# Attention's softmax denominators from one running sum over four key blocks

## The chip, the cores and the metric

The kernel runs on one core of a Trainium2 chip. The metric is device time in microseconds, the median of several runs; smaller is better. Engines are called as the profile calls them: PE is TensorE, DVE is VectorE, ACT is ScalarE, POOL is GpSimd, SP is SyncE (here it only issues DMAs).

## The reference

The program is a masked self-attention followed by a routed and a shared feed-forward layer. The change touches the attention alone:

```python
def _L0_cond_ref(x, mask, Wq, Wo):          # x: (16, 256, 512), mask: (16, 512)
    NH = 8
    B, D, T = x.shape
    dk = D // NH                            # 32
    xt = jnp.transpose(x, (0, 2, 1))
    q = xt @ Wq.T
    qh = q.reshape(B, T, NH, dk).transpose(0, 2, 1, 3)
    scores = scale * jnp.einsum('bhqd,bhkd->bhqk', qh, qh)
    logits = (scores * cmask + (1.0 - cmask) * NEG) * rmask
    attn = jax.nn.softmax(logits, axis=-1)
    ctx = jnp.einsum('bhqk,bhkd->bhqd', attn, qh)
    ...
x = x + _L0_ffn_ref(_L0_cond_ref(x, cond_2048, Wq, Wo), ...)
```

The softmax needs, for each query, the sum of exp(logit - max) over the 512 keys. That sum is the denominator of which this text tells.

## The kernel before

The program has three stages that follow one another: attention (about the first 735 us of the span), experts, shared.

Attention works in 32 units (NU): a unit u is one batch element and four of its eight heads (HG = 4). The keys of a unit are taken in KB = 4 blocks of 128. Scores are held transposed, keys on the partitions and the 512 queries along the row, so the sum over keys is a sum over partitions and over the four blocks.

For each unit, key block kb and head g:
- PE makes the scores of the block (`ps_e`, L557), and, for the unit two further on, the product whose row maximum is wanted (`ps_m`, L562). Both use two banks in turn, g % 2.
- ACT takes the exponential of `ps_e` into the tile `e[kb]` (L337), 512 queries by four heads, 2048 elements in a row.
- DVE takes the maximum of `ps_m` into `maxcol` (L420). PE may be at most two `ps_m` products ahead of it.
- PE multiplies `e[kb]` with the values into `ps_num` (`numerators`, L455): four products, which the trace shows as eight. They are issued one block late: those of block kb stand in block kb + 1, behind its head 1, and those of block 3 in block 0 of the next unit.

The denominators: `add_pair` adds e[1] into e[0] on POOL (all four heads, 2048 elements), and e[3] into e[2], half of the heads (1024 elements) on DVE and half on POOL. PE then multiplies e[0] with ones into `ps_den` (`denominators(u, 0)`, behind the last head of block 3 of the same unit), and e[2] in the same way on top of it (`denominators(u - 1, 1)`, behind the last head of block 1 of the next unit). ACT copies `ps_den` to `den`, DVE takes the reciprocal in four parts in blocks 2 and 3 of that next unit (L386) and then makes c_f = num * den (L391), all in SBUF. Behind c_f, in even units, DVE copies the small logits tile from PSUM to SBUF (L430). At the start of an even unit it makes two rows of the mask, `row_mask` and `row_neg` (L411, L412), one partition of 512 elements each, from SBUF to SBUF.

Every engine runs its own list of instructions strictly in order; what couples them are the semaphores. POOL's list in the step of unit u is: its half of the last add of unit u - 1; c_lo of unit u - 2 (L232, waits for ACT's c_hi, which waits for c_f); the add of e[1] into e[0] (L148); q_lo, qm_hi, qm_lo for the unit four further on (L243, L244, L246, 512 elements each); in odd steps x_lo (L251, 1024 elements). SP's list waits for qm_lo before it issues the next load of x and the next eight stacking DMAs. In odd steps PE makes two groups of six output products (L444), in even steps the transposes and small products of the routing logits. Both kinds of step have one group of six for q (L444).

The order on DVE, written out in its `step`: in blocks 0 to 3 a maximum for each head; behind head 1 of block 1 its half of the last add of unit u - 1; behind heads 1 and 3 of blocks 2 and 3 the reciprocals; behind the last one c_f.

Of the kernel before, what the change touches and what calls it, by code (L numbers as in the profile page):

```python
def attention(nc, ctx, sems, keep, x, mask, wqT, woT, gates, attn):
# [88 lines left out]
    maxrow_in = [sem(f"maxrow_in{n}") for n in range(RING)]  # L90
    stored = [sem(f"stored{n}") for n in range(2)]
    e_mm, m_mm, num_mm, den_mm = sem("e_mm"), sem("m_mm"), sem("num_mm"), sem("den_mm")
    pair_dve, pair_pool = sem("pair_dve"), sem("pair_pool")
    q_mm, v_mm, mt_mm, o_mm = sem("q_mm"), sem("v_mm"), sem("mt_mm"), sem("o_mm")
    e_done, q_done, v_done, mt_done = sem("e_done"), sem("q_done"), sem("v_done"), sem("mt_done")
    num_done, den_done, chi_done, o_done = sem("num_done"), sem("den_done"), sem("chi_done"), sem("o_done")
# [41 lines left out]
            return lo <= RING * i + n + off < hi  # L138
        return True

    def add_pair(eng, u, pair, heads, done):

        k = 2 * pair

        eng.wait_ge(e_done, (KB * u + k + 2) * HG)
        eng.wait_ge(num_mm, KB * u + k + 1)
        into = e[k][:, heads, :]
        eng.tensor_tensor(into, into, e[k + 1][:, heads, :], ALU.add).then_inc(done, 1)  # L148

    block = ctx.enter_context(nc.Block())  # L150

# [60 lines left out]
    def _(pool):  # L212
# [11 lines left out]
        def step(i, n):  # L224
            u = RING * i + n
            if known(i, n, -1):
                add_pair(pool, u - 1, 1, slice(HG // 2, HG), pair_pool)
            if known(i, n, -2):
                w, slot = u - 2, (n - 2) % RING

                upto(pool, chi_done, w + 1)
                pool.tensor_tensor(c_lo[slot][:], c_f[n % 2][:], c_hi[slot][:], ALU.subtract).then_inc(c_split, 1)  # L232
            if known(i, n):
                add_pair(pool, u, 0, slice(0, HG), pair_pool)
            if known(i, n, 4):
                w, par, bp = u + 4, n % 2, n // 2

                upto(pool, q_done, 2 * (w + 1))
                pool.wait_ge(mask_in[bp], 16 * (i + 2))

                if known(i, n, 2):
                    upto(pool, stack_in[(n + 2) % RING], 16 * STACK_DMAS * (i + 1 + (n + 2) // RING))
                pool.tensor_tensor(q_lo[par][:], q_f[par][:], q_hi[par][:], ALU.subtract).then_inc(ql_done, 1)  # L243
                pool.tensor_tensor(qm_hi[par][:], q_hi[par][:], mask_b[bp][:], ALU.mult).then_inc(ql_done, 1)  # L244
                upto(pool, ql_done, 2 * (w + 1))
                pool.tensor_tensor(qm_lo[par][:], q_lo[par][:], mask_b[bp][:], ALU.mult).then_inc(q_split, 1)  # L246
            if n % 2 == 1 and known(i, n, 5):
                w = 2 * i + (n + 5) // 2
                bp = (n + 5) // 2 % 2
                pool.wait_ge(xhi_done, w + 1)  # L250
                pool.tensor_tensor(x_lo[:], x_f[bp][:], x_hi[:], ALU.subtract).then_inc(x_split, 1)  # L251
# [6 lines left out]
    def _(act):  # L258
# [5 lines left out]

        def copy_denominators(i, n):
            w, par = RING * i + n - 1, (n - 1) % 2
            act.wait_ge(den_mm, 2 * (w + 1))
            act.activation(den[par][:], ps_den[:, :], ACT.Copy).then_inc(den_done, 1)  # L268

        def context_high(i, n):  # L270
# [59 lines left out]

        def weights(i, n, kb, g):
            u = RING * i + n
            if g == 0 and kb % 2 == 0:

                upto(act, den_mm, 2 * (u - 1) + 1 + kb // 2)
            act.wait_ge(e_mm, (KB * u + kb) * HG + g + 1)
            act.activation(e[kb][:, g, :], ps_e[g % 2][:, :], ACT.Exp, scale=SCALE).then_inc(e_done, 1)  # L337

# [36 lines left out]
    def _(dve):  # L375
# [27 lines left out]
        def step(i, n):  # L403
# [9 lines left out]
            for kb in range(KB):  # L413
                for g in range(HG):
                    if known(i, n, 2):
                        w, par = u + 2, n % 2
                        dve.wait_ge(m_mm, (KB * w + kb) * HG + g + 1)
                        if kb == 0 and g == 0:
                            upto(dve, mt_mm, w - 1)
                        dve.reduce_max(maxcol[par][:, g * KB + kb:g * KB + kb + 1], ps_m[g % 2][:, :], AX.X).then_inc(max_done, 1)  # L420
                    if g == 1 and kb == 1 and known(i, n, -1):
                        add_pair(dve, u - 1, 1, slice(0, HG // 2), pair_dve)
                    if g % 2 == 1 and known(i, n, -1):
                        normalise(i, n, 2 * kb + g // 2 - KB)
                        if kb == KB - 1 and g == HG - 1:
                            normalise(i, n, PARTS)
# [9 lines left out]
    def _(pe):  # L436
# [19 lines left out]
                                        start=(kb == 0), stop=(kb == KB - 1))  # L456
            last.then_inc(num_mm, 1)

        def denominators(u, pair):

            if pair == 0:

                upto(pe, den_done, u)
            if pair == 1:
                pe.wait_ge(pair_dve, u + 1)
            pe.wait_ge(pair_pool, 2 * u + pair + 1)
            for g in range(HG):
                last = nc.tensor.matmul(ps_den[g * DK:(g + 1) * DK, :], ones[:, :], e[2 * pair][:, g, :],
                                        start=(pair == 0), stop=(pair == 1))
            last.then_inc(den_mm, 1)  # L470

        def turn_values(i, n):
# [65 lines left out]
        def step(i, n):  # L538
# [6 lines left out]
            for kb in range(KB):  # L545
# [7 lines left out]
                for g in range(HG):  # L553
# [23 lines left out]
                    if g == 2 and kb >= 2 and n % 2 == 1 and known(i, n, -3, hi=NU):  # L577
                        out_rows(i, n, kb - 2)
                    if g == 3 and kb == 1 and known(i, n, -1):
                        denominators(u - 1, 1)  # L580
                    if g == 3 and kb == 3 and known(i, n):
                        denominators(u, 0)

        run_units(pe, step, -4, 5)

# [821 lines left out]
```

## Time and profile before

| what | value |
|---|---|
| median of the runs | 2069.23 us (2065.56 to 2070.95, 3 runs) |
| span of the profiled execution | 2067.4 us |
| busy over the whole span | PE 93%, DVE 51%, ACT 35%, POOL 29% |
| busy in 300 to 500 us, inside attention | PE 96%, DVE 82%, ACT 67%, POOL 64% |

Shares over the whole span mix three stages. The attention stage is read from its own stretch, and what sets its pace from the order of time on each engine. A row of the order of time has start, duration, engine, line, operation, tiles; in square brackets stands how long the engine was idle before it and which engine and tile let it go.

### The profile page before, as it was taken

To read this page: it belongs to the slowest core of one execution; us is meant where nothing else is said; L and a number is where in the kernel's file an instruction comes from. 1 tells how busy PE (TensorE), PEld (TensorE's weight loads), DVE (VectorE), ACT (ScalarE), POOL (GpSimd) and SP (SyncE) were. 2 spreads that over 40 slices of the span, in tenths; PEclk is the share of its full clock that TensorE was granted. 3 is DMA by queue.
4 is the path that set the end of the run, shared out by engine and by line. 5 is a ranking of instruction groups with operands and counts; after the bars stand their busy time and mean duration, and the time that the engine had idled before them with its cause. 6 is when DMAs were issued, how large, how long until landed. Compare 5 with 4: busy or idle time off the path is not lost. (4 is left out here: it accounts for less than half of the span.)

```text
span 2067.4 us, 30281 instructions
## 1 busy us (share of the span) xinstructions
PE 1920.6 (93%) x10324; PEld 1418.9 (69%) x10325; DVE 1061.5 (51%) x1723; ACT 720.1 (35%) x1282; POOL 591.3 (29%) x433
## 2 busy tenths in 40 slices
PE   4999999999999836999999999799999999999996
PEld 2444444444444326999999999688888888888885
DVE  3788888787888455344443443444233332424333
ACT  1566666666666512324343332311101010101100
POOL 3556665666565413111111111001010100101010
PEclk9899999999999956999999999899999999999998
DMA  7765757576765033233332322523030211203021
GB/s 126 120 111 98 113 102 125 92 113 95 131 84 73 21 143 125 81 116 110 123 121 73 114 80 81 169 91 102 1 102 20 81 51 51 67 34 101 0 81 41
DMA packets 103041, 184.22 MB, mean 89 GB/s; under 512 B 10560, under 2 KB 31040, under 8 KB 102992
## 3 DMA queue, kind: packets, MB, share of 16 engines
q1 hardware_dynamic: 91952, 147.41, 32.3%
q0 software_dynamic: 11040, 36.18, 5.9%
q8 instruction: 28, 0.46, 0.1%
q14 instruction: 21, 0.17, 0.0%
HBM read 92.03 MB, written 40.37 MB: 64 GB/s over the span
## 5 line engine op out<-in xcount | busy, mean ns | idle before, releaser
L420 DVE TENSOR_REDUCE maxcol<-ps_m 128x1 f32<-128x512 f32 x512 | 337.5, 681 | 138.8 <-PE ps_m L562 133.1
L337 ACT ACTIVATE e<-ps_e 128x512 f32<-128x512 f32 x512 | 297.0, 596 | 188.4 <-PE ps_e L557 187.6
L1234 DVE TENSOR_TENSOR s_h_f<-s_silu,s_ps_u 128x512 f32<-128x512 f32 x88 | 60.6, 688 | 450.6 <-PE s_ps_u L1290 399.1
L148 POOL TENSOR_TENSOR e<-e 128x2048 f32<-128x2048 f32 x64 | 225.6, 3524 | 181.8 <-ACT e L337 181.5
L1202 ACT ACTIVATE s_silu<-s_ps_g 128x512 f32<-128x512 f32 x88 | 52.6, 598 | 608.1 <-PE s_ps_g L1290 600.5
L562 PE MATMUL ps_m<-kside,qside 97*128 97x512 f32 x512 | 224.7, 444 | 33.2 <-DVE maxcol L420 18.9
L1177 POOL DMA_INDIRECT s_chosen<-routed,s_slot_now x64 | 61.0, 952 | 670.0 <-DVE s_total L1265 659.4
L557 PE MATMUL ps_e<-qside,kside 98*128 98x512 f32 x512 | 237.7, 467 | 3.2 <-ACT e L337 2.4
L557 PEld LDWEIGHTS ps_e<-qside,kside 98*128 98x128 f32 x512 | 97.2, 191 | 192.3 <-ACT e L337 159.1
L964 DVE TENSOR_TENSOR e_h_f<-e_silu,e_ps_h 128x256 f32<-128x256 f32 (+1 forms) x108 | 45.1, 418 | 249.0 <-ACT e_silu L831 249.0
L562 PEld LDWEIGHTS ps_m<-kside,qside 97*128 97x128 f32 x512 | 101.0, 197 | 78.9 <-DVE maxcol L420 53.9
L1290 PE MATMUL s_ps_g<-s_x_hi,s_gu_hi 128*128 128x512 f32 x352 | 138.4, 393 | 3.6 <-DVE s_d_lo L1223 3.6
L455 PE MATMUL ps_num<-e,v 128*32 128x512 f32 x1024 | 137.9, 611 | 0.1
L1290 PE MATMUL s_ps_g<-s_x_lo,s_gu_hi 128*128 128x512 f32 x352 | 137.7, 391 | 0.0
L1301 PE MATMUL s_ps_y<-s_d_hi,s_h_hi 128*128 128x512 f32 x352 | 137.7, 391 | 0.0
L1290 PE MATMUL s_ps_g<-s_x_hi,s_gu_lo 128*128 128x512 f32 x352 | 137.6, 391 | 0.0
L1301 PE MATMUL s_ps_y<-s_d_hi,s_h_lo 128*128 128x512 f32 x352 | 137.1, 389 | 0.0
L1301 PE MATMUL s_ps_y<-s_d_lo,s_h_hi 128*128 128x512 f32 x352 | 136.9, 389 | 0.0
L1290 PE MATMUL s_ps_u<-s_x_hi,s_gu_hi 128*128 128x512 f32 x352 | 136.9, 389 | 0.0
L1290 PE MATMUL s_ps_u<-s_x_lo,s_gu_hi 128*128 128x512 f32 x352 | 136.9, 389 | 0.0
L1290 PE MATMUL s_ps_u<-s_x_hi,s_gu_lo 128*128 128x512 f32 x352 | 136.9, 389 | 0.0
L386 DVE RECIPROCAL den<-den 128x128 f32<-128x128 f32 x128 | 119.5, 939 | 17.0 <-ACT den L268 17.0
(203 smaller groups left out, 4040.8 us busy)
## 6 DMA issues: line engine op xcount, KB each, us to landing
routed<-e_y SPq DMA_DIRECT2D x36, 512.0 KB, 2.8
kside<-q_hi SPq DMA_DIRECT2D x64, 256.0 KB
qside<-qm_hi SPq DMA_DIRECT2D x64, 256.0 KB
x_f<-in_x SPq DMA_DIRECT2D x16, 512.0 KB, 3.4
kside<-q_lo SPq DMA_DIRECT2D x32, 256.0 KB
qside<-qm_lo SPq DMA_DIRECT2D x32, 256.0 KB
attn<-xo SPq DMA_DIRECT2D x32, 256.0 KB, 3.3
keep_rows<-attn SPq DMA_DIRECT2D x8, 1024.0 KB, 5.6
```

The lines of the kernel that those rows point to most:

```text
L148: eng.tensor_tensor(into, into, e[k + 1][:, heads, :], ALU.add).then_inc(done, 1)
L337: act.activation(e[kb][:, g, :], ps_e[g % 2][:, :], ACT.Exp, scale=SCALE).then_inc(e_done, 1)
L386: dve.reciprocal(den[par][:, c], den[par][:, c]).then_inc(rd_done, 1)
L420: dve.reduce_max(maxcol[par][:, g * KB + kb:g * KB + kb + 1], ps_m[g % 2][:, :], AX.X).then_inc(max_done, 1)
L455: last = nc.tensor.matmul(ps_num[g * DK:(g + 1) * DK, :], v[n % RING][:, kb, g, :], e[kb][:, g, :], start=(kb == 0), stop=(kb == KB - 1))
L557: nc.tensor.matmul(ps_e[g % 2][:, :], kside[n][:, g, cols], qside[n][:, g, :], start=True, stop=True).then_inc(e_mm, 1)
L562: nc.tensor.matmul(ps_m[g % 2][:, :], qside[s2][0:MAXROW, g, cols], kside[s2][0:MAXROW, g, :], start=True, stop=True).then_inc(m_mm, 1)
L1177: pool.indirect_dma_start(out=chosen[k][s % 2][:], out_offset=None, in_=routed, in_offset=bass.IndirectOffsetOnAxis(ap=slot_now[:, k, s:s ...
L1202: act.activation(silu[:], ps_g[:], ACT.Silu).then_inc(silu_done, 1)
L1234: dve.tensor_tensor(h_f[:], silu[:], ps_u[:], ALU.mult).then_inc(h_done, 1)
L1290: last = nc.tensor.matmul(ps[:], l[:, t, k, m, :], r[:, m, :], start=(c == 0), stop=(c == len(terms) - 1))
L1301: last = nc.tensor.matmul(ps_y[s][:], l[t % 2][:, c], r[:, t, :], start=(t == 0 and m == 0), stop=(t == NI - 1 and m == 2))
```

## The change

One running sum takes the place of two pair sums. e[0] is added into e[1], that into e[2], that into e[3]. The first two adds are POOL's, all four heads. The last is split between DVE and POOL as the second pair was. PE multiplies e[3] alone with ones: one group of denominators instead of two, in the place of the later one. POOL's first add stands where it stood, but now waits for the numerators of block 1 (before: of block 0), since it writes e[1]. Its second add stands behind the three q operations, ahead of x_lo. The last add, on both engines, waits for the second. ACT waits for the sums before it writes the tiles of the next unit.

```diff
-    def add_pair(eng, u, pair, heads, done):
-        k = 2 * pair
-        eng.wait_ge(e_done, (KB * u + k + 2) * HG)
-        eng.wait_ge(num_mm, KB * u + k + 1)
-        into = e[k][:, heads, :]
-        eng.tensor_tensor(into, into, e[k + 1][:, heads, :], ALU.add).then_inc(done, 1)
+    def add_next(eng, u, kb, heads, done):
+        eng.wait_ge(e_done, (KB * u + kb + 1) * HG)
+        eng.wait_ge(num_mm, KB * u + kb + 1)
+        if kb > 1:
+            eng.wait_ge(sum_pool, (KB - 1) * u + kb - 1)
+        into = e[kb][:, heads, :]
+        eng.tensor_tensor(into, into, e[kb - 1][:, heads, :], ALU.add).then_inc(done, 1)
...
             if known(i, n, -1):
-                add_pair(pool, u - 1, 1, slice(HG // 2, HG), pair_pool)
+                add_next(pool, u - 1, 3, slice(HG // 2, HG), sum_pool)
...
             if known(i, n):
-                add_pair(pool, u, 0, slice(0, HG), pair_pool)
+                add_next(pool, u, 1, slice(0, HG), sum_pool)
...
                 pool.tensor_tensor(qm_lo[par][:], q_lo[par][:], mask_b[bp][:], ALU.mult).then_inc(q_split, 1)
+            if known(i, n):
+                add_next(pool, u, 2, slice(0, HG), sum_pool)
...
-            act.wait_ge(den_mm, 2 * (w + 1))
+            act.wait_ge(den_mm, w + 1)
...
-            if g == 0 and kb % 2 == 0:
-                upto(act, den_mm, 2 * (u - 1) + 1 + kb // 2)
+            if g == 0 and kb < KB - 1:
+                upto(act, sum_pool, (KB - 1) * (u - 1) + kb + 1)
+            if g == 0 and kb == KB - 2:
+                upto(act, sum_dve, u)
+            if g == 0 and kb == KB - 1:
+                upto(act, den_mm, u)
...
-                        add_pair(dve, u - 1, 1, slice(0, HG // 2), pair_dve)
+                        add_next(dve, u - 1, 3, slice(0, HG // 2), sum_dve)
...
-        def denominators(u, pair):
-            if pair == 0:
-                upto(pe, den_done, u)
-            if pair == 1:
-                pe.wait_ge(pair_dve, u + 1)
-            pe.wait_ge(pair_pool, 2 * u + pair + 1)
+        def denominators(u):
+            upto(pe, den_done, u)
+            pe.wait_ge(sum_dve, u + 1)
+            pe.wait_ge(sum_pool, (KB - 1) * (u + 1))
             for g in range(HG):
-                last = nc.tensor.matmul(ps_den[g * DK:(g + 1) * DK, :], ones[:, :], e[2 * pair][:, g, :],
-                                        start=(pair == 0), stop=(pair == 1))
+                last = nc.tensor.matmul(ps_den[g * DK:(g + 1) * DK, :], ones[:, :], e[KB - 1][:, g, :], start=True, stop=True)
             last.then_inc(den_mm, 1)
...
                     if g == 3 and kb == 1 and known(i, n, -1):
-                        denominators(u - 1, 1)
-                    if g == 3 and kb == 3 and known(i, n):
-                        denominators(u, 0)
+                        denominators(u - 1)
```

## Rows read from the trace of the kernel before

**Rows 1.** Stages: window, length, busy of each engine, PEclk, DMA share, GB/s.

```profile
300.00:500.00 200.00, 192.30 (x1033) 94.79 (x1032) 164.32 (x226) 134.46 (x249) 128.15 (x64) 0.99 0.66 107
```

**Rows 2.** Order of time, PE, 400 to 445: start, duration, what, idle before.

```profile
405.90 1.06 PE L455 MATMUL ps_num<-e,v 128*32 128x512 f32 x8
...
422.12 1.06 PE L468 MATMUL ps_den<-e,ones 128*32 128x512 f32 x8
...
425.64 1.06 PE L455 MATMUL ps_num<-e,v 128*32 128x512 f32 x8
...
433.42 0.40 PE L557 MATMUL ps_e<-qside,kside 98*128 98x512 f32 x1
433.65 0.40 PE L562 MATMUL ps_m<-kside,qside 97*128 97x512 f32 x1
433.98 1.06 PE L468 MATMUL ps_den<-e,ones 128*32 128x512 f32 x8
...
435.32 0.40 PE L562 MATMUL ps_m<-kside,qside 97*128 97x512 f32 x1
...
438.86 0.50 PE L562 MATMUL ps_m<-kside,qside 97*128 97x512 f32 x1 [0.80 <-DVE maxcol L420]
...
443.73 1.07 PE L468 MATMUL ps_den<-e,ones 128*32 128x512 f32 x8
```

**Rows 3.** Order of time, DVE, around two unit boundaries.

```profile
415.15 1.77 DVE L391 TENSOR_TENSOR c_f<-num,den 128x512 f32<-128x512 f32 x1
...
435.68 1.86 DVE L391 TENSOR_TENSOR c_f<-num,den 128x512 f32<-128x512 f32 x1
...
438.13 3.85 DVE L420 TENSOR_REDUCE maxcol<-ps_m 128x1 f32<-128x512 f32 x6
```

**Rows 4.** Order of time, POOL, the odd unit.

```profile
428.34 1.28 POOL L243 TENSOR_TENSOR q_lo<-q_f,q_hi 128x512 fp32r<-128x512 f32 x1 [0.97 <-ACT q_hi L301]
...
430.94 1.29 POOL L246 TENSOR_TENSOR qm_lo<-q_lo,mask_b 128x512 fp32r<-128x512 f32 x1
...
434.61 2.38 POOL L148 TENSOR_TENSOR e<-e 128x1024 f32<-128x1024 f32 x1
```

**Rows 5.** Order of time, POOL, the boundary behind unit 1.

```profile
99.25 2.38 POOL L251 TENSOR_TENSOR x_lo<-x_f,x_hi 128x1024 fp32r<-128x1024 f32 x1
101.59 2.80 POOL L148 TENSOR_TENSOR e<-e 128x1024 f32<-128x1024 f32 x1
104.34 1.45 POOL L232 TENSOR_TENSOR c_lo<-c_f,c_hi 128x512 fp32r<-128x512 f32 x1
```

**Rows 6.** Order of time, DVE, the same boundary behind unit 1.

```profile
100.65 1.53 DVE L391 TENSOR_TENSOR c_f<-num,den 128x512 f32<-128x512 f32 x1
102.10 2.57 DVE L411 CAST row_mask<-mask_b 1x512 fp32r<-1x512 f32 x1
...
105.99 1.27 DVE L420 TENSOR_REDUCE maxcol<-ps_m 128x1 f32<-128x512 f32 x2
```

**Rows 7.** Groups by form, POOL, 200 to 600: count, busy, mean ns, idle before.

```profile
L148 POOL TENSOR_TENSOR e<-e 128x2048 f32<-128x2048 f32 x19 | 87.3, 4594 | 82.8 <-ACT e L337 82.8
L148 POOL TENSOR_TENSOR e<-e 128x1024 f32<-128x1024 f32 x20 | 47.6, 2381 | 14.4 <-ACT e L337 14.1
```

**Rows 8.** Order of time, PE, unit 1 and the boundary behind it.

```profile
92.71 1.06 PE L455 MATMUL ps_num<-e,v 128*32 128x512 f32 x8
...
106.72 0.79 PE L562 MATMUL ps_m<-kside,qside 97*128 97x512 f32 x1 [3.99 <-DVE maxcol L420]
...
112.83 1.07 PE L468 MATMUL ps_den<-e,ones 128*32 128x512 f32 x8
```

**Rows 9.** Stages, two microseconds behind that boundary; columns as in rows 1.

```profile
106.00:108.00 2.00, 1.28 (x4) 0.91 (x5) 1.71 (x4) 0.00 (x0) 0.00 (x0) 0.50 1.10 157
```

**Rows 10.** Order of time, POOL, the last unit's last add.

```profile
711.87 3.38 POOL L148 TENSOR_TENSOR e<-e 128x1024 f32<-128x1024 f32 x1 [4.08 <-ACT e L337]
```

**Rows 11.** Order of time, PE, the last unit's denominators.

```profile
715.40 1.07 PE L468 MATMUL ps_den<-e,ones 128*32 128x512 f32 x8 [1.80 <-POOL e L148]
```

More of the change, by code:

```diff
@@ L92, in attention @@
     e_mm, m_mm, num_mm, den_mm = sem("e_mm"), sem("m_mm"), sem("num_mm"), sem("den_mm")
-    pair_dve, pair_pool = sem("pair_dve"), sem("pair_pool")
+    sum_dve, sum_pool = sem("sum_dve"), sem("sum_pool")
     q_mm, v_mm, mt_mm, o_mm = sem("q_mm"), sem("v_mm"), sem("mt_mm"), sem("o_mm")
```

## Prediction, made before the change was run

> **What bounds the kernel now.** I read the profile in this order: busy time by stage, the costliest groups, then the order of time on TensorE (PE), VectorE (DVE) and GpSimd (POOL) over two units, and last two odd places, in the first and the last units. Only the attention stage, the first third of the span, is touched. In its middle PE is busy 192.3 of 200 us at a granted clock of 0.99, DVE 164, ScalarE 134, POOL 128 [rows 1]. So PE looks like the bound, and POOL looks like the engine with room. Units repeat in pairs, an even and an odd one, of 41.4 us: 19.74 us from the even unit's key block 1 numerators (405.90) to the odd one's (425.64), and back 21.61, read between the denominator groups at 422.12 and 443.73 [rows 2].
>
> The order of time says where PE's share misleads. Behind the last max product of an odd unit (433.65) comes PE's first denominator group (433.98), one more pair of products, and then a product that waited 0.80 us for DVE's maximum, at 438.86 [rows 2]. DVE at that place goes through c_f = num/den, two mask rows and only then the first maximum of the next unit, 438.13 [rows 3]. That chain hangs on nothing that PE does between 433.65 and 438.86. So at each unit boundary DVE is the last to come, and PE already waits.
>
> The second thing to see is c_f. It takes 1.86 us at 435.68 [rows 3], while POOL's 1024-element add runs from 434.61 to 436.99 [rows 4]: c_f ends 0.55 us after POOL does. The same in the early place: c_f issued at 100.65 takes 1.53 us and ends at 102.18, 0.55 us behind the end of POOL's x_lo (99.25 + 2.38 = 101.63) [rows 5, 6]. So a DVE operation with two inputs in SBUF stands still while POOL runs an add, and the other way round: the POOL add queued right behind x_lo takes 2.80 us instead of 2.38 (+0.42) [rows 5]. At the handoff DVE, which had been waiting, went first, although POOL's next instruction was already queued. Then the mask row takes 2.57 us and the next maximum starts at 105.99: both mask operations lost one POOL instruction each [rows 5, 6]. They take 0.59 us together where POOL is idle (end of c_f at 437.54 to 438.13 [rows 3]).
>
> **The change, part by part.** I time each unit from T, the start of its key block 1 numerators: 425.64 for the odd unit, 405.90 for the even one [rows 2].
>
> *Removed: one denominator group of PE per unit.* Max product to max product across it is 435.32 - 433.65 = 1.67 us; two ordinary steps of 0.23 (433.42 to 433.65) would be 0.46, so the group costs 1.21 us [rows 2]. 32 units give 38.7 us of PE time. But it stands at the boundary, before the product that waits for DVE. It comes off the wait and not off the period: I count it at nothing. What hides it is the chain c_f, masks, first maximum.
>
> *Added: one more 2048-element add of POOL per unit, and the first moved later.* POOL's 2048 add is 4.59 us, the 1024 one 2.38 [rows 7]. The first add now waits for key block 1's numerators, T + 1.06 + about 0.1 = T+1.15, where it waited for block 0's. It ends at T+5.74. Behind it, moved 3 us, stand the three q operations, 3.89 us (428.34 to 430.94 + 1.29) [rows 4]: they end at T+9.63. Their stacking DMAs and the load of x on SP's queue wait for the last of them; the stacks are wanted a unit later, so I count nothing, and if that cover were gone it would be the 3 us once per unit. Then the new add: T+9.63 to T+14.22. Then x_lo (2.38, odd units only), POOL's half of the last add (2.38), c_lo. ScalarE's new waits (weights of block 0 for the first sum, block 1 for the second, and so on) end before the ones reckoned below, except in even units by less than a microsecond, and there PE waits for the denominators anyway.
>
> *Odd unit into even unit.* c_f is ready at 435.68 - 425.64 = T+10.04. The new add has been running since T+9.63, so c_f stands until T+14.22 and ends about 0.55 later. Then the pattern of the early place [rows 5, 6] returns: POOL takes x_lo, the first mask row stands behind it; POOL takes its half of the last add, the second mask row stands behind that. In the early place 4.36 us went from POOL's end (101.63) to the first maximum (105.99) [rows 5, 6] with two POOL instructions of 2.38 and 1.29 in them, so 0.69 over them. Here: 14.22 + 2.38 + 2.38 + 0.69 = T+19.67, against 438.13 - 425.64 = T+12.49 now: +7.2 us. PE, already waiting there, takes all of it. It will stand for some 9 us. In the early place it stood 3.99 us before 106.72 [rows 8], the granted clock behind that was 0.50, the level of 1.2 GHz [rows 9], and from its restart to the denominators took 112.83 - 106.72 = 6.11 us [rows 8], against 443.73 - 438.86 = 4.87 now [rows 2]: +1.2 us. Sum +8.4 us. This happens for odd units 3 to 25, 12 times: 101 us. Unit 1 has no output products yet, so its c_f is ready at 100.65 - 92.71 = T+7.94 [rows 6, 8] and meets the second q operation; the first mask row stands behind the third, the second behind the new add, which ends near 107.5: first maximum at 107.7 where it is 105.99 now, +1.7. After unit 27 there are no masks and no x_lo any more: c_f alone, from T+11.9 to T+14.8, +2.8.
>
> *Even unit into odd unit.* c_f is ready at 415.15 - 405.90 = T+9.25 [rows 2, 3], within the last q operation, which ends at T+9.63. DVE goes first, c_f ends at T+10.18, 0.8 us sooner than now (415.15 + 1.77, T+11.02). The new add loses 0.42 and ends at T+14.64. Both halves of the last add need it, DVE's and POOL's, and they cannot run side by side: in the last unit they start together and the POOL half takes 3.38 instead of 2.38, and the denominators start 715.40 - 711.87 = 3.53 us after that add began [rows 10, 11]. So the denominators come at 14.64 + 0.1 + 3.53 = T+18.27 against 422.12 - 405.90 = T+16.22: +2.05 us, and the 0.8 won is lost in it. 14 such units: 28.7 us.
>
> *Last units (28 to 31).* No q operations, so the new add starts earlier; the removed group is worth 1.21 us in two of them, the last unit's sums are serial and give about 2 us back. Zero, with 5 us either way.
>
> Sum: 101 + 1.7 + 2.8 + 28.7 = 134 us. On the profiled span of 2067.4 that is 2201; the median of the runs is 1.8 above it: **2203 us**.
>
> No row shows the logits copy of even units (PSUM to SBUF, after c_f) beside a POOL add. If it stood too it would cost the even boundary: c_f T+10.2, copy behind the new add at about T+14.8, denominators 5.2 us later at T+20.0 instead of 18.27, +1.7 x 14 = +24 us. Below nothing it can't be. I take zero, since the maxima, which also read PSUM, do not slow beside POOL. The Trainium skill's "VectorE: DVE Perf Modes", section "Why PSUM operands drop a tier", says that the mode of DVE which uses both SBUF read ports is closed to a PSUM operand; by it the price is zero too.
>
> For the handoff the Trainium skill's "SBUF — State Buffer", section "Who interferes with whom", says that issue order decides and the later one blocks fully. It doesn't say who goes next when both have something queued; row 101.59 says DVE [rows 5]. By issue order alone POOL's queued add would be as good a candidate, and that is rival B.
>
> **The rivals.**
> A. c_f gets in ahead of the new add in odd units. The margin is T+10.04 against T+9.63. Then the add ends near T+15.1, the first mask row follows it, the second follows x_lo: first maximum at about T+18.0, 1.6 us less each: 2203 - 19 = 2184.
> B. POOL's queue wins the handoffs. Odd: DVE comes in after x_lo and the last add, T+19.0 + 1.2, +0.5 more than forecast; even: c_f waits through the new add and POOL's half, ends T+17.2, denominators 5.2 later, T+22.4, 4.1 us more. 12 x 0.5 + 14 x 4.1 = 64: 2267. Against it: the add of 101.59, which lost 0.42 us to the waiting c_f [rows 5].
> C. The logits copy stands as well: 2227.
> D. No standing still, only POOL's longer chain: odd T+14.22 + 2.38 + 2.38 + 0.1 = T+19.1 against 18.1 now, +1.0 x 13; even T+16.7 against 16.2, +0.5 x 14: +20, 2089. Against it: c_f's 1.86 us [rows 3].
> E. **Faster**: PE's 96% is what counts and the removed group comes off whole: 2069 - 39 = 2030. Its place is the unit boundary; it decides if DVE's chain there is shorter than PE's, which needs the first maximum to start by T+10.5: PE without its wait and the group would be at the product of 438.86 at 436.85, T+11.2, and a maximum takes 0.7. For it: PE's share [rows 1]. Against it: the 0.80 us that PE waits there already [rows 2], and POOL's 4.6 us right on c_f.
> F. PE's saving turns into wait and nothing else changes: 2069.
>
> **How the numbers follow.** Forecast 0.60, with its own range 2166 to 2236 (12 odd boundaries from 6 to 9.5 us each, clock included, even ones from 1.5 to 3.5). A 0.08, B 0.07, C 0.08, D 0.07, E 0.06, F 0.04. The range of eight in ten takes in the forecast, A, B and C: 2140 to 2268; D, E and F are left out, 0.17. A measurement of this kernel can tell about 0.3% from no change. Faster: 0.06. Same: 0.04. Slower: the rest, 0.90.
>
> **What would show it.** In the changed profile: c_f in odd units near 4.7 us instead of 1.86, and 0.9 in even ones; the first mask row about 2.5 us, the second as long; PE's max product behind the boundary idle some 8 to 9 us before it, by DVE, in odd units; the granted clock at 0.50 after each; POOL's 2048 adds twice as many; the even unit's denominator group waiting 2 to 3 us for the adds; two units taking about 51.8 us instead of 41.4; DVE's half of the last add between 1.2 and 3.5 us. Wrong would be: c_f under 2 us in odd units (D or A), or a first maximum before T+13. The forecast falls with the margin of 0.4 us between the new add and c_f, with the handoff going to POOL, or with a clock that stays down past the denominators (more than 1.2 us per boundary).

## The result, and the profile after

The changed kernel takes 2242.82 us, median of four runs (2241.13 to 2243.49); the kernel before, beside it, 2068.91. The ratio is 1.0843, 95% interval 1.0828 to 1.0857: 174 us slower. The prediction was 2203 us, 134 us slower, with a range of 2140 to 2268. The direction, the mechanism and that range held. The loss was sized 40 us too small: the time lies 7 us above the forecast's own, narrower range of 2166 to 2236, and inside the outer one only because that left room for rival B (2267), which did not come about in this kernel. So that the range held is in part luck. This text is mostly about those 40 us and about a few places where my picture was too simple.

The stage first. A stretch inside attention, columns as in rows 1:

```profile
340.00:540.00 200.00, 150.75 (x742) 78.56 (x740) 153.31 (x177) 105.65 (x195) 146.51 (x59) 0.89 0.50 85
```

PE fell from 192.3 to 150.8 busy of 200 us [rows 1], though it has less to do; DVE from 164 to 153; POOL rose from 128 to 147. The granted clock fell from 0.99 to 0.89. No engine is near full: they wait for one another.

The order of time on PE, an odd unit (T = 414.55) into an even one (T = 444.89):

```profile
411.02 1.06 PE L471 MATMUL ps_den<-e,ones 128*32 128x512 f32 x8 [1.55 <-POOL e L148]
...
414.55 1.07 PE L461 MATMUL ps_num<-e,v 128*32 128x512 f32 x8
...
425.24 0.50 PE L559 MATMUL ps_e<-qside,kside 98*128 98x512 f32 x1
434.89 0.80 PE L564 MATMUL ps_m<-kside,qside 97*128 97x512 f32 x1 [9.15 <-DVE maxcol L426]
...
441.37 1.06 PE L471 MATMUL ps_den<-e,ones 128*32 128x512 f32 x8
...
444.89 1.07 PE L461 MATMUL ps_num<-e,v 128*32 128x512 f32 x8
...
463.06 1.85 PE L471 MATMUL ps_den<-e,ones 128*32 128x512 f32 x8 [1.54 <-POOL e L148]
```

The wait of 0.80 us [rows 2] has become 9.15, and the even unit's denominators, which waited for nothing, now wait 1.54 us for POOL's sum.

DVE, from the end of an even unit to the next even one:

```profile
402.10 0.97 DVE L397 TENSOR_TENSOR c_f<-num,den 128x512 f32<-128x512 f32 x1
402.99 0.16 DVE L436 COPY keep_logits<-ps_o 128x18 f32 x1
...
407.52 1.23 DVE L148 TENSOR_TENSOR e<-e 128x1024 f32<-128x1024 f32 x1 [0.61 <-POOL e L148]
...
424.55 4.73 DVE L397 TENSOR_TENSOR c_f<-num,den 128x512 f32<-128x512 f32 x1
429.20 2.56 DVE L417 CAST row_mask<-mask_b 1x512 fp32r<-1x512 f32 x1
431.69 2.55 DVE L418 TENSOR_SCALAR row_neg<-mask_b 1x512 fp32r<-1x512 f32 x1
434.17 1.27 DVE L426 TENSOR_REDUCE maxcol<-ps_m 128x1 f32<-128x512 f32 x2
```

POOL beside it:

```profile
415.79 4.59 POOL L148 TENSOR_TENSOR e<-e 128x2048 f32<-128x2048 f32 x1 [3.59 <-PE ps_num L461]
...
422.97 1.29 POOL L246 TENSOR_TENSOR qm_lo<-q_lo,mask_b 128x512 fp32r<-128x512 f32 x1
424.22 4.51 POOL L148 TENSOR_TENSOR e<-e 128x2048 f32<-128x2048 f32 x1
428.69 2.79 POOL L253 TENSOR_TENSOR x_lo<-x_f,x_hi 128x1024 fp32r<-128x1024 f32 x1
431.44 2.52 POOL L148 TENSOR_TENSOR e<-e 128x1024 f32<-128x1024 f32 x1
433.92 1.44 POOL L232 TENSOR_TENSOR c_lo<-c_f,c_hi 128x512 fp32r<-128x512 f32 x1
```

Read the two together. The new add starts at 424.22, 0.33 us ahead of c_f. c_f ends at 429.28, 0.55 us behind the end of that add. Each mask row, 0.41 us of work, then stands behind one POOL instruction, and each POOL instruction that follows is 0.14 to 0.4 us longer for having let DVE in first. Compare rows 3 to 6: the pattern that stood once in the kernel before, behind unit 1, now stands behind 12 odd units.

### The profile page after: what moved, and what is told of

It reads as the page before. It is cut to its first block and busy times, and to the rows that moved or that the text cites. A ratio compares the mean times of both kernels' runs of the same rounds, so it can differ in the third digit from the quotient of the medians.

```text
span 2241.2 us, 29944 instructions
## 1 busy us (share of the span) xinstructions
PE 1935.1 (86%) x10068; PEld 1440.1 (64%) x10069; DVE 1155.9 (52%) x1723; ACT 721.7 (32%) x1282; POOL 762.9 (34%) x465
## 5 line engine op out<-in xcount | busy, mean ns | idle before, releaser
L148 POOL TENSOR_TENSOR e<-e 128x2048 f32<-128x2048 f32 (+1 forms) x96 | 392.8, 4092 | 245.5 <-PE ps_num L461 242.9
L564 PE MATMUL ps_m<-kside,qside 97*128 97x512 f32 x512 | 237.1, 468 | 146.4 <-DVE maxcol L426 132.5
L559 PE MATMUL ps_e<-qside,kside 98*128 98x512 f32 x512 | 250.6, 491 | 21.5 <-ACT e L343 20.1
L559 PEld LDWEIGHTS ps_e<-qside,kside 98*128 98x128 f32 x512 | 104.5, 205 | 210.6 <-ACT e L343 151.0
L564 PEld LDWEIGHTS ps_m<-kside,qside 97*128 97x128 f32 x512 | 109.7, 214 | 189.8 <-DVE maxcol L426 163.0
L461 PE MATMUL ps_num<-e,v 128*32 128x512 f32 x1024 | 148.8, 656 | 0.8 <-ACT e L343 0.7
L781 POOL COPY e_now<-e_token_of 128x2 uint32 (+1 forms) x37 | 8.4, 226 | 375.8 <-PE e_ps_t L1000 374.2
```

The source lines that it names most:

```text
L148: eng.tensor_tensor(into, into, e[kb - 1][:, heads, :], ALU.add).then_inc(done, 1)
L461: last = nc.tensor.matmul(ps_num[g * DK:(g + 1) * DK, :], v[n % RING][:, kb, g, :], e[kb][:, g, :], start=(kb == 0), stop=(kb == KB - 1))
L559: nc.tensor.matmul(ps_e[g % 2][:, :], kside[n][:, g, cols], qside[n][:, g, :], start=True, stop=True).then_inc(e_mm, 1)
L564: nc.tensor.matmul(ps_m[g % 2][:, :], qside[s2][0:MAXROW, g, cols], kside[s2][0:MAXROW, g, :], start=True, stop=True).then_inc(m_mm, 1)
```

## The experiments

Eleven kernels, each timed beside the kernel before; ratios are to it, with 95% intervals.

**The kernel before with one denominator group of PE less** (before_one_group). The prediction had counted the removed group at nothing, since it stood in front of a wait.

```diff
-            if g == 0 and kb % 2 == 0:
-
-                upto(act, den_mm, 2 * (u - 1) + 1 + kb // 2)
+            if g == 0 and kb == 0:
+                upto(act, pair_pool, 2 * (u - 1) + 1)
+            if g == 0 and kb == 2:
+                upto(act, den_mm, u)
...
                     if g == 3 and kb == 1 and known(i, n, -1):
                         denominators(u - 1, 1)
-                    if g == 3 and kb == 3 and known(i, n):
-                        denominators(u, 0)
```

With the group some waits change too, as the first lines show, and ACT's copy adds 0.001.

> The kernel before with its first denominator group of PE taken out alone: POOL and DVE add as before, and the product with e[2] stands alone. It leaves key blocks 0 and 1 out of the denominators, and adds 0.001 to them so that none is zero. My theory: the group (1.21 us, 32 times) stood in front of a product that waits for DVE's chain anyway, so its time turns into wait: 2069 us, within 6 us. Rival (PE's share of 96% is what counts): 2069 - 39 = 2030 us. In the profile the product behind the odd boundary would wait 2.0 us for DVE instead of 0.80.

Measured: 2088.96 us, ratio 1.0095 (1.0075 to 1.0116). Neither theory had this: with less to do on PE the kernel is 20 us slower. Its trace, PE behind an odd boundary, and the stages behind it:

```profile
392.92 1.07 PE L456 MATMUL ps_num<-e,v 128*32 128x512 f32 x8
...
406.11 0.51 PE L560 MATMUL ps_m<-kside,qside 97*128 97x512 f32 x1 [1.97 <-DVE maxcol L421]
408.60 1.94 PE L456 MATMUL ps_num<-e,v 128*32 128x512 f32 x8
412.53 1.07 PE L466 MATMUL ps_den<-e,ones 128*32 128x512 f32 x8
```

```profile
404.00:406.00 2.00, 0.14 (x1) 0.00 (x0) 2.00 (x5) 1.08 (x2) 0.62 (x2) 1.00 1.07 290
...
408.00:410.00 2.00, 2.00 (x10) 0.38 (x9) 1.93 (x3) 2.00 (x4) 0.00 (x0) 0.54 1.08 131
```

DVE in the same place:

```profile
405.38 4.01 DVE L421 TENSOR_REDUCE maxcol<-ps_m 128x1 f32<-128x512 f32 x6
```

The wait is 1.97 us instead of 0.80, as expected: the group's 1.2 us did turn into wait. The first maximum stays where it was, at T+12.46 (405.38 - 392.92) against T+12.49 before. But the granted clock, 1.00 in the place of rows 2, is then at 0.54, next to its level of 1.2 GHz, and the numerators group takes 1.94 us instead of 1.06. Over 200 us (340 to 540) the granted clock is 0.95 here against 0.99. It does not fall behind every such wait: here it stays at 1.00 from 348 to 408 us, through waits of 1.99 and 1.44. And once, behind its 0.80 us wait at 395.94, it falls in the kernel before as well (0.50 from 398 to 400).

**The same with five idle products in that place** (one_group_filler). Against before_one_group this puts back PE's activity, and nothing else but PE's wait for the copy of the denominators; the changed waits stay.

```diff
+                    if g == 3 and kb == 3 and known(i, n):
+                        upto(pe, den_done, u)
+                        for r in range(5):
+                            nc.tensor.matmul(ps_den[:, :], wo_hi[:, 0, 0:P], wo_hi[:, :, :].rearrange("p k d -> p (k d)"), start=True, stop=True)
```

> The kernel before_one_group (2089 us) with five products of 128x512 (weights by weights, 1.17 us together) in the place of the removed denominators group. Like it, this kernel leaves key blocks 0 and 1 out of the denominators. Nothing but PE's activity at the boundary is put back. My theory (the removed group cost 20 us by letting PE stand 2.0 us instead of 0.8 behind boundaries, after which the granted clock fell to 0.50): the low stretches go and the time comes back to 2069, within 6 us. Rival (the loss comes from the other waits that this kernel changed): 2089 us.

Measured: 2068.36 us, ratio 1.0001 (0.9991 to 1.0010). The 20 us are gone although the changed waits are still there, and the granted clock is back at 1.00: what cost them was the quiet on PE and the low clock behind it. That the removed product's time is worth nothing at the boundary is shown by before_one_group, where the first maximum did not move. The same 200 us stretch:

```profile
340.00:540.00 200.00, 191.79 (x1009) 104.62 (x1005) 163.90 (x226) 134.79 (x250) 130.63 (x64) 1.00 0.67 108
```

**The changed kernel, PE kept busy through the long wait** (after_filler).

```diff
+                    if g == 2 and kb == 0 and n % 2 == 0 and known(i, n, 0, lo=4, hi=27):
+                        pe.wait_ge(o_done, KT * (2 * i + (n - 4) // 2 + 1))
+                        for r in range(34):
+                            nc.tensor.matmul(ps_o[:, :], wo_hi[:, 0, 0:P], wo_hi[:, :, :].rearrange("p k d -> p (k d)"), start=True, stop=True)
                     if known(i, n, 2):
                         s2 = (n + 2) % RING
```

> The changed kernel with 34 products of 128x512 (weights by weights into a free bank, about 0.23 us each, 7.9 us together) ahead of the product that waits 9.15 us behind odd units 3 to 25: PE works through the wait instead of standing. No other engine does anything else. My theory (part of the loss above the forecast is the clock at 1.2 GHz after the long wait, and it lasts past the denominators): the stretches at 0.50 behind odd boundaries go, from restart to denominators 4.9 us instead of 6.5 to 7.2, and the second low stretch in even units may go with them: 12 x 1.6 to 12 x 3.5 less, 2200 to 2224 us. Rival (the clock costs nothing there, DVE is last): 2243 us; if the filler is itself too long, above that.

Measured: 2228.30 us, ratio 1.0766 (1.0747 to 1.0785), 14.5 us less than the changed kernel. In its trace:

```profile
314.55 7.90 PE L563 MATMUL ps_o<-wo_hi 128*128 128x512 f32 x34
324.02 0.50 PE L568 MATMUL ps_m<-kside,qside 97*128 97x512 f32 x1 [1.57 <-DVE maxcol L426]
...
328.90 1.06 PE L471 MATMUL ps_den<-e,ones 128*32 128x512 f32 x8
```

From restart to denominators 4.88 us, as in the kernel before (4.87 [rows 2]). The gain is less than the 19 to 42 us expected, because this is not so everywhere: from an even unit's denominators to the next odd unit's it takes 28.9 us where the clock holds, which it does in two of the twelve places, and 30.3 or 32.1 in the others. Low stretches stayed behind some of the waits of 1.57 us that the filler leaves open, and behind even units, where PE waits for about 1 and 1.5 us.

**Filler at both waits** (after_filler_both): in addition nine products into `ps_den` ahead of the denominators of even units.

```diff
-        def denominators(u):
+        def denominators(u, fill):
...
             upto(pe, den_done, u)
+            if fill:
+                for r in range(9):
+                    nc.tensor.matmul(ps_den[:, :], wo_hi[:, 0, 0:P], wo_hi[:, :, :].rearrange("p k d -> p (k d)"), start=True, stop=True)
             pe.wait_ge(sum_dve, u + 1)
...
-                        denominators(u - 1)
+                        denominators(u - 1, n % 2 == 1 and known(i, n, -1, lo=2, hi=28))
```

> The changed kernel with filler products at both waits: 34 ahead of the 9.15 us wait behind odd units (as in after_filler), and 9 (2.1 us) ahead of the denominators of even units, which wait 1.55 us for POOL. My theory (what is left over the forecast's waits is the clock alone): units 2 to 27 run at 1.0, an odd to even stretch is 28.9 us and an even to odd one 21.8: 12 x 7.2 + 13 x 2.05 + 8 = 121 us over the kernel before, 2190 to 2200 us; the 9 products may hold the denominators some tenths longer than the wait was. Rival (the low stretches of even units cost nothing, only the odd ones do): as after_filler, 2228 us.

Measured: 2213.08 us, ratio 1.0698 (1.0677 to 1.0719). 2190 to 2200 was expected. The middle of attention is as expected, the ends are not. Its clock there:

```profile
340.00:540.00 200.00, 184.77 (x944) 107.69 (x940) 159.31 (x184) 108.69 (x203) 146.39 (x58) 1.00 0.56 90
```

A pair of units takes 51.1 us there (denominators at 378.19 and 429.26, two odd units), of which 0.4 is filler longer than the wait it fills (the even unit's denominators start 0.46 us behind the end of POOL's add, 0.05 in the changed kernel); 50.7 at full clock against 41.4 before. In the changed kernel a pair takes 53.6 on average (denominators of units 5 and 25 at 228.95 and 764.73, ten pairs). So the clock is worth 2.9 us per pair. PE's wait of 1.57 us behind odd units is as long here as in after_filler, and there the clock fell behind most of them; here, with the even units' wait filled, it held at 1.00 throughout these 200 us. So one wait of that length alone doesn't bring it down; the quiet around it counts too. The low stretches ahead of 148 us and behind 776 us, most of them without filler, stayed, and one at 576 to 584 us.

**The mask rows out of the way** (after_masks_late): the two instructions stand behind DVE's half of the last add.

```diff
-            if n % 2 == 0 and known(i, n, 4):
-                ...
-                dve.tensor_copy(row_mask[bp][:], mask_b[bp][0:1, :]).then_inc(rows_done, 1)
-                dve.tensor_scalar(row_neg[bp][:], mask_b[bp][0:1, :], -NEG, NEG, ALU.mult, ALU.add).then_inc(rows_done, 1)
...
                     if g == 1 and kb == 1 and known(i, n, -1):
                         add_next(dve, u - 1, 3, slice(0, HG // 2), sum_dve)
+                    if g == 1 and kb == 1 and n % 2 == 0 and known(i, n, 4):
+                        ...
```

> The changed kernel with DVE's two mask rows moved from the start of even units to behind DVE's half of the last add (key block 1). My theory (each mask operation stands behind one POOL instruction of 2.4 us, and PE with them): the first maximum behind the odd boundary starts at T+14.8 instead of T+19.7, PE's wait falls from 9.15 us to about 4.2; 4.9 us less in 12 units, and some more if the low clock ends sooner: 2175 to 2185 us. Rival (the masks only stretch because c_f is late, and the denominators hold PE anyway): 2230 to 2243 us.

Measured: 2175.72 us, ratio 1.0532 (1.0501 to 1.0563), 67 us less than the changed kernel. As expected: in its new place a mask row takes 0.41 us, PE's wait behind odd units is 4.17 us.

**c_f with one input in PSUM** (after_c_from_psum).

```diff
-                dve.reciprocal(den[par][:, c], den[par][:, c]).then_inc(rd_done, 1)
+                dve.reciprocal(ps_den[:, c], ps_den[:, c]).then_inc(rd_done, 1)
...
-                dve.tensor_tensor(c_f[par][:], num[par][:], den[par][:], ALU.mult).then_inc(c_done, 1)
+                dve.tensor_tensor(c_f[par][:], num[par][:], ps_den[:, :], ALU.mult).then_inc(c_done, 1)
...
-                    copy_denominators(i, n)
...
-            upto(pe, den_done, u)
+            upto(pe, c_done, u)
```

> The changed kernel with c_f reading the reciprocal from PSUM: the four reciprocals work in place on the denominators' bank, ACT's copy of them goes, and c_f has one input in SBUF. The group of the next unit waits for c_f. My theory (two SBUF inputs are what makes c_f stand): c_f takes about 0.7 us in odd units although the second add runs, but the first mask row then stands behind that add and the second behind x_lo: first maximum at T+17.0 instead of T+19.7, 2.6 us less in 12 units and 0.4 in 14: 2206 us. Rival A (each stall counts by itself, c_f's 4.1 us are simply gone): 2193 us. Rival B (c_f stands behind POOL whatever its operands): 2243 us.

Measured: 2183.11 us, ratio 1.0553 (1.0535 to 1.0570). DVE in an odd unit, T = 346.37:

```profile
356.38 0.69 DVE L396 TENSOR_TENSOR c_f<-num,ps_den 128x512 f32<-128x512 f32 x1
356.99 3.85 DVE L416 CAST row_mask<-mask_b 1x512 fp32r<-1x512 f32 x1
360.77 2.55 DVE L417 TENSOR_SCALAR row_neg<-mask_b 1x512 fp32r<-1x512 f32 x1
363.25 1.27 DVE L425 TENSOR_REDUCE maxcol<-ps_m 128x1 f32<-128x512 f32 x2
```

c_f no longer stands, though POOL's add ran from 356.04 to 360.56: two inputs in SBUF are what makes it stand, and rival B of this expectation is out. The next in line, the mask row, stands in its stead, and the first maximum comes at T+16.9 (17.0 expected). So stalls on one chain don't add: taking one away uncovers the next. The time still fell by 60 us and not by 37; behind the shorter wait fewer stretches at the low clock are seen (granted clock over 200 to 700 us 0.91 against 0.89), but I have not separated the two.

**Both together** (after_both).

> The changed kernel with c_f from PSUM and the masks behind DVE's half of the last add: nothing of DVE stands at the boundary. Left are the removed group and POOL's longer chain, whose two last halves exclude each other. My theory: first maximum at about T+10.7 in odd units, but the denominators wait for POOL: T+20.2 instead of 18.1 in odd units, T+17.9 instead of 16.2 in even ones, 3.7 us per pair, 48 us: 2117 us, up to 2140 with stretches at 1.2 GHz. Rival (with the stall gone the removed product pays): 2030 to 2060 us.

Measured: 2169.18 us, ratio 1.0468 (1.0436 to 1.0501), 52 us more than expected. The boundary is free, PE waits there 0.19 us. The loss moved to the denominators of odd units. DVE, then POOL, then PE:

```profile
361.71 6.77 DVE L148 TENSOR_TENSOR e<-e 128x1024 f32<-128x1024 f32 x1
```

```profile
361.49 2.39 POOL L253 TENSOR_TENSOR x_lo<-x_f,x_hi 128x1024 fp32r<-128x1024 f32 x1
363.83 2.36 POOL L148 TENSOR_TENSOR e<-e 128x1024 f32<-128x1024 f32 x1
366.13 1.28 POOL L232 TENSOR_TENSOR c_lo<-c_f,c_hi 128x512 fp32r<-128x512 f32 x1
```

```profile
368.72 1.94 PE L470 MATMUL ps_den<-e,ones 128*32 128x512 f32 x8 [4.77 <-DVE e L148]
```

DVE's half of the last add stood behind three POOL instructions in a row and ran only when POOL's queue was empty. This is the handoff of rival B of the prediction. It went so in 9 of the 12 odd units 3 to 25 (6.67 to 6.81 us); in the other three DVE got in behind x_lo (3.25 to 3.27 us). DVE had come 0.18 to 0.32 us after x_lo began in the nine and 0.21 to 0.22 in the three, so that does not tell them apart. In the changed kernel c_f, the first mask row and the second came 0.33, 0.40 and 0.24 us or more after the start of a POOL instruction and always got in at its end; so did, in even units of after_second_add_ahead_of_q, a DVE add that came 0.07 us after. What decides is open.

**The last add on DVE alone** (after_both_last_add_on_dve).

```diff
...
-                add_next(pool, u - 1, 3, slice(HG // 2, HG), sum_pool)
...
-                        add_next(dve, u - 1, 3, slice(0, HG // 2), sum_dve)
+                        add_next(dve, u - 1, 3, slice(0, HG), sum_dve)
```

> As after_both, and the last add wholly on DVE (2048 elements, 2.4 us) with none of it on POOL. My theory (the two halves exclude each other, so 1.2 + 2.4 us in a row is worse than 2.4 on DVE alone): denominators at T+17.0 in both kinds of unit, 1 to 3 us per pair less than after_both: 2080 to 2100 us. Rival (DVE has no room for 1.2 us more per unit): at or above after_both.

Measured: 2158.82 us, ratio 1.0431 (1.0414 to 1.0449): 10 us better than after_both, and 59 above the top of the expected 2080 to 2100, in part for the same reason. The add, 2.29 us alone, takes 5.5 us behind x_lo and c_lo in six of the twelve odd units 3 to 25, 4.3 us behind x_lo alone in the other six, and 3.3 us behind c_lo in even units.

**Another place for the long add** (after_second_add_ahead_of_q): the same instructions, POOL's second add ahead of the q operations.

```diff
             if known(i, n):
                 add_next(pool, u, 1, slice(0, HG), sum_pool)
+                add_next(pool, u, 2, slice(0, HG), sum_pool)
...
-            if known(i, n):
-                add_next(pool, u, 2, slice(0, HG), sum_pool)
```

> The changed kernel with POOL's second add ahead of the three q operations: the same work on every engine, only the place of the 4.6 us add differs. It then runs from T+5.9 to T+10.5 and c_f (ready at T+10.04) stands 0.5 us instead of 4.2; the mask rows stand behind q operations of 1.3 us instead of instructions of 2.4. My theory (the place of the long add is what costs): first maximum at T+13.8 instead of T+19.7, then the denominators wait for POOL's last add: 2.6 us per odd and 2.1 per even unit over the kernel before, 2130 us, to 2150 with the low clock. The stacking loads start 5 us later and could make PE wait at a unit's start. Rival (the amount of POOL's work counts, not its place): 2230 to 2243 us.

Measured: 2168.73 us, ratio 1.0507 (1.0468 to 1.0546), against 2130 to 2150 expected. The amount of work is the same and 74 us went, so its place is what mattered. c_f takes 1.27 us in odd units, the mask rows 1.48 each, PE waits 3.5 us at that boundary. The expected side effect came too: PE waits for a load 9 times between 200 and 700 us, 9.0 us in all; the q operations, and with them the stacks, come later here. The trace shows one more thing that the estimate left out. In even units c_f now meets the long add (2.07 us at 370.86 instead of 0.97), and the two halves of the last add start together:

```profile
376.70 3.38 DVE L148 TENSOR_TENSOR e<-e 128x1024 f32<-128x1024 f32 x1
```

The denominators of even units wait 2.1 us for that add. How much of the excess each of these is worth I have not taken apart.

**The long add in two halves** (after_second_add_halved): two instructions of 1024 elements for the one of 2048.

```diff
...
+        if kb == 2:
+            for lo in range(0, HG, HG // 2):
+                into = e[kb][:, lo:lo + HG // 2, :]
+                last = eng.tensor_tensor(into, into, e[kb - 1][:, lo:lo + HG // 2, :], ALU.add)
+                last.then_inc(done if lo else half_done, 1)
+            return
```

> The changed kernel with POOL's second add issued as two of 1024 elements: the same elements and almost the same POOL time, with a handoff in the middle. My theory (DVE gets in at the end of the POOL instruction that runs when it arrives): in odd units c_f stands until T+12.0 instead of T+14.2, the first mask row then behind the second half, the second behind x_lo: first maximum at T+17.4 instead of T+19.7, 2.3 us less in 12 units, 2215 us, or a few us less. Rival (DVE gets in only when POOL's queue is empty): c_f stands as long as before and nothing is won: 2243 us.

Measured: 2213.80 us, ratio 1.0707 (1.0689 to 1.0725), 29 us less than the changed kernel, 2215 expected. c_f in odd units:

```profile
362.27 2.56 DVE L403 TENSOR_TENSOR c_f<-num,den 128x512 f32<-128x512 f32 x1
364.75 2.56 DVE L423 CAST row_mask<-mask_b 1x512 fp32r<-1x512 f32 x1
```

2.56 us instead of 4.73: in this kernel, as in the changed one, c_f stands for the rest of the one POOL instruction that runs when it arrives. (The DVE adds of after_both show that this is not so for every instruction.)

**The kernel before, with its own collision removed** (before_add_behind_c_lo). The change didn't invent the collision: c_f, 0.69 us where nothing is in its way, lost 1.2 us to it before and loses 4.0 now. So the other direction is open too: POOL's half of the last add behind c_lo.

```diff
...
-            if known(i, n, -1):
-                add_pair(pool, u - 1, 1, slice(HG // 2, HG), pair_pool)
             if known(i, n, -2):
                 ...
                 pool.tensor_tensor(c_lo[slot][:], c_f[n % 2][:], c_hi[slot][:], ALU.subtract).then_inc(c_split, 1)
+            if known(i, n, -1):
+                add_pair(pool, u - 1, 1, slice(HG // 2, HG), pair_pool)
```

> The kernel before with one change of order on POOL: its half of the last add stands behind c_lo, not ahead of it, so that it no longer runs when DVE's c_f is ready. My theory (DVE's two-input operation stands still while POOL runs an add, and DVE's chain sets the boundary): c_f takes 0.7 us instead of 1.8, PE's waits of 0.80 and 0.22 us behind the boundaries go, 1.0 us per pair of units, about 14 pairs: 2054 us, at best 2069 - 32 x 1.1 = 2034 if DVE's chain were all. Rival (c_f's length is not on the path): 2069 us. It also tells whether POOL's half, now about 4 us later, holds the denominators: then slower than 2069.

Measured: 2044.85 us, ratio 0.9886 (0.9869 to 0.9902): 23 us faster than the kernel before, and the fastest of all. DVE behind an odd unit, and the stage:

```profile
380.74 0.69 DVE L391 TENSOR_TENSOR c_f<-num,den 128x512 f32<-128x512 f32 x1
381.35 0.41 DVE L411 CAST row_mask<-mask_b 1x512 fp32r<-1x512 f32 x1
```

```profile
340.00:540.00 200.00, 196.46 (x1074) 98.53 (x1070) 161.56 (x236) 139.97 (x260) 132.00 (x65) 1.00 0.71 112
```

c_f takes 0.69 us instead of 1.86 [rows 3] and PE is busy 196.5 of 200 us; it doesn't wait for a maximum any more. The gain is 23 us where 15 were expected: a pair takes 40.0 us (denominators at 387.75 and 427.77) instead of 41.4, 1.4 us less where 1.0 was reckoned from PE's two waits. Where the rest comes from I have not taken apart.

## Why the prediction was right, and where it was off

*The bound.* That DVE's chain at the unit boundary sets the pace, not PE's 96%, is shown by before_one_group (a PE group less, the first maximum still at T+12.46, the wait 1.17 us longer) together with one_group_filler, which takes out the clock's part (ratio 1.0001), and from the other side by before_add_behind_c_lo (1.2 us off c_f, 1.1% faster).

*Odd into even.* Forecast: c_f ready at T+10.04 behind the new add, first maximum at T+19.67. Measured: c_f at T+10.00, 4.73 us long, first maximum at 434.17, T+19.62. PE's wait 9.15 us, "some 9" forecast. after_masks_late, after_c_from_psum and after_second_add_halved moved it by what the handoffs say.

*Even into odd.* Forecast: c_f 0.9 us long, denominators at T+18.27. Measured: 0.97, and 463.06 - 444.89 = T+18.17. The two halves of the last add did run one after the other: DVE's from 407.52 to 408.75, POOL's until 410.97. PE's wait for them was 1.55 us, less than the 2 to 3 forecast; ahead of it PE waited 1.09 us for ACT, at 408.26, which the prediction had put at less than a microsecond.

*The logits copy.* Rival C is out: the copy takes 0.16 us at 402.99, beside POOL's add:

```profile
402.48 8.49 POOL L148 TENSOR_TENSOR e<-e 128x2048 f32<-128x2048 f32 x2
```

The Trainium skill's "VectorE: DVE Perf Modes", section "Why PSUM operands drop a tier", says that the mode which needs both SBUF read ports is not open to a PSUM operand. The row agrees.

*The handoff.* Right for the changed kernel: c_f stood, 4.70 to 4.73 us, behind the new add in all thirteen odd units from 3 to 27, and DVE went next. It failed as a general rule: the expectation of after_both rested on it, and the run met rival B's handoff in nine units of twelve. The one place it was taken from [rows 5, 6] showed it for c_f and a mask row. For these it held in every kernel here; for a DVE add no row had shown it.

*The term that was mis-sized: the clock.* The step that failed is the +1.2 us per odd unit, from "from its restart to the denominators took 112.83 - 106.72 = 6.11 us", taken from the one place where PE had stood 3.99 us. It measures 2.9 us per pair. Two things were missed. The restart costs more here: 434.89 to 441.37 is 6.48 us, and 221.76 to 228.95 in another unit 7.19. And the clock comes down behind even units as well, for which the prediction has no term. It had named this as a way to fail, a "clock that stays down past the denominators". The waits without the clock were sized right: 41.4 + 7.2 + 2.05 = 50.65 us for a pair, and 50.7 measured at full clock in after_filler_both. The changed kernel behind even units 8 and 12, both two microseconds long:

```profile
304.00:306.00 2.00, 2.00 (x8) 1.28 (x5) 0.29 (x1) 1.19 (x2) 0.00 (x0) 0.50 1.07 126
...
412.00:414.00 2.00, 2.00 (x13) 1.62 (x10) 0.69 (x1) 1.09 (x2) 0.20 (x1) 1.00 1.07 127
```

The second row lies behind the denominators at 411.02: there the clock held, and the stretch from those denominators to the next is 30.35 us (411.02 to 441.37). Behind the first it did not, and the stretch is 32.39 (302.65 to 335.04). Nine of the twelve are of the longer kind. At full clock, with filler at both waits, it is 28.95 (400.31 to 429.26).

*The account.* Starts of the denominators of odd units, changed less before:

| stretch | before, us | after, us | more | forecast |
|---|---|---|---|---|
| start to unit 1 | 112.83 | 120.15 | 7.3 | 3.8 |
| unit 1 to 3 | 39.75 | 54.54 | 14.8 | 10.4 |
| unit 3 to 25, 11 pairs | 456.35 | 590.04 | 133.7 | 115 |
| unit 25 to 27 | 40.53 | 48.75 | 8.2 | 4.8 |
| unit 27 to 31 | 65.94 | 72.93 | 7.0 | 0 |
| rest of the span | 1351.98 | 1354.79 | 2.8 | 0 |
| sum | 2067.4 | 2241.2 | 173.8 | 134 |

Of the 40 us missed, 18.7 lie in the eleven middle pairs, and there the clock's 2.9 us per pair against the 1.2 forecast makes 11 x 1.7 = 18.7. Filler took away 14.5 us with the long wait filled, and 15.2 more with the even units' wait filled as well. The other 21 us lie at the ends. There the low clock is seen too (0.66 over 90 to 100 us, 1.00 in the kernel before), but I put no filler in, so for them the clock is argued and not shown. The last four units, taken as zero, cost 7 us: without q operations the new add starts sooner, but c_f meets it all the same, 2.82 us long at 857.73 and 4.20 at 874.10, where it was 0.69 to 1.78 before. That was a slip of the sum, not of the mechanism; how much of the 7 us is c_f and how much the clock, which is low there too, is open. The 2.8 us behind attention are open as well.

*The removed group.* "I count it at nothing" is right at full clock only. Taken alone it costs 20 us through the clock. In the changed kernel I take that for no term of its own, since PE stands 9 us at the odd boundary in any case; this is argued, no run of the changed kernel has the group back.

## What to carry to other kernels

Before giving an idle engine more to do, look at what the new instruction will stand beside: a POOL add of 4.6 us that began 0.3 us ahead of one DVE multiply cost it 4.0 us at each odd unit (4.73 against 0.69), and two mask rows behind it lost 4.3 us more. The cheap cures are order, not amount: one line moved on POOL's list in the kernel before gave 1.1%, and the same long add issued elsewhere or in two halves gave back 74 and 29 us. And work taken off PE in front of a wait can be worth less than nothing: watch the granted clock behind each wait that gets longer.

## What the runs showed of the hardware that I had not expected

- PE work removed made the kernel slower: 1.2 us less of PE per unit, 20 us more in total, with waits of 1.4 to 2.0 us in place of 0.2 to 0.8 behind boundaries and the granted clock at 0.95 instead of 0.99; idle products in the same place bring back 2068.36 us.
- A DVE add with two SBUF inputs that came 0.2 to 0.3 us after POOL's x_lo began lost the next handoffs 9 times of 12 and stood until POOL had ended all three instructions in a row (6.8 us for an add of 1.2 us). In the changed kernel c_f and the mask rows, 0.24 us or more after a POOL instruction's start, always got in at its end.
- Mask rows on one partition, 0.41 us from SBUF to SBUF with a single input, stand behind a POOL add as a 128-partition multiply does (2.56 us). A multiply with one input in PSUM (0.69 us), a copy from PSUM (0.16) and the maxima from PSUM (0.69) don't.
